# Newton-Schulz inverse: five squaring steps, or a factored geometric sum of powers

## The chip, the cores and the metric

The kernel is one program on one core of a Trainium2 chip. The metric is the device time of one execution in microseconds. The engines are TensorE (PE in the profile, with its weight loads as PEld), VectorE (DVE), ScalarE (ACT), GpSimd (POOL) and the DMA queues, most of them issued by SyncE (SP). Every engine executes its own instruction list in order; they are tied together by semaphores that are written out by hand.

## The reference, cut to what matters

Four residual blocks follow one another on x of shape 8 x 16 x 128 x 128 in float32 (batch, channel, row, column):

```
x = x + conv3x3(_gn(x), L0_weights) + bias        # conv A
x = x + newton_inverse(_gn(x), 5)                 # 128 matrices of 128 x 128
x = x + circular_conv3x3(_gn(x), L2_weight)       # conv C, written as an FFT
x = x + conv3x3(_gn(x), L3_K), last row/col zero  # conv D

def newton_inverse(W, 5):                         # per matrix, n = 128
    X = W^T / (max column abs sum * max row abs sum)
    5 times:  X = X (2I - W X)
```

_gn normalizes over pairs of channels and all pixels. With R = I - W X at the start, five Newton steps give X times the sum of R^k for k from 0 to 31. That sum is what both kernels compute, in different factorings.

## The kernel before, in words

One turn of the main loop (a cycle, `pe_cycle`, `dve_cycle`, ... with index i from 0 to 7) handles batch i's inverse and, beside it, convs of its neighbours: conv A of batch i+1, conv C and conv D of batch i-1. Cycles 0, 1, 6 and 7 are written out, cycles 2 to 5 are a hardware loop. The 16 matrices of a batch are four chunks of four (NMAT = 4); a chunk is one SBUF or PSUM tile of 128 x 512. A round works on two chunks, s = 0 and 1, in turn, so that TensorE has one chunk's products while the other's results are copied out.

The order of TensorE in a cycle is: transposes of the matrices and the Gram products of chunks 0 and 1 (`pe_norms`, lines 721 and 704), conv C of batch i-1 in six groups, **round 0**, conv A of batch i+1 in six groups, **round 1**, conv D of batch i-1 in six groups. A conv group is 9 matmuls (27 rows of a profile line marked x27 are three groups), and needs weights `w` and the high and low parts `d` of the window, which ScalarE (line 531, high) and VectorE (line 503, low) write.

A round before has five steps. `R` holds the residual matrix: step k squares it on TensorE (line 752), ScalarE copies the square from PSUM to the other R buffer (line 825), TensorE multiplies V with R (line 759), and VectorE adds the product to V (line 947 in step 0 with the scale, line 953 in steps 1 to 3, line 958 in step 4, which writes x2). Step 4 squares nothing; in round 0 it holds the Gram products of chunks 2 and 3 instead (line 704). A chunk thus takes 4 squarings, 5 products with V and 1 Gram.

GpSimd multiplies V by the scale before step 0 (line 1136, four instructions), and adds V to the kept x1 after step 3 (line 1128), since the last product is added to U = V + x1.

The order around the rounds is fixed by hand. Between the steps VectorE does side work for the neighbouring convs: statistics of the next windows (`win_stats_1`, `_2`, `_3`, lines 432 to 481), the square root's refinement of four small dependent instructions (lines 379 to 383), the conv weights (lines 494 to 496), and low parts. After round 1 it takes the statistics of x2 (line 553), on which the weights of conv C hang, while x2 goes to DRAM and comes back as windows of conv C.

## Time and profile before

| what | value |
|---|---|
| median of 3 runs | 698.43 us (694.57 to 700.22) |
| profiled execution: its span from first to last instruction | 696.2 us |
| TensorE busy | 621.8 us, 89% |
| VectorE busy | 543.7 us, 78% |
| ScalarE busy | 280.2 us, 40% |
| GpSimd busy | 198.3 us, 28% |
| one cycle of the loop, start of round 0 to the next | 78.3 us |

The profiled execution has no separate time in the results beside its span; the span lies 2.2 us under the median of the runs. In the timeline a row is start, duration, engine, line, operation, the tiles out<-in, and in brackets the idle time before it with what ended it. Rows of one kind that follow closely are merged (x4), and then the duration is that of the whole. A float32 matmul is counted as two rows in PE, so that one product of a chunk (four matmuls) is x8.

### The profile page before, as it was taken

Reading aid. Unit: us, or ns where it says so; the run is one execution under the profiler, and the core shown is the slowest. Engines: PE = TensorE matmul, PEld = TensorE weight load, DVE = VectorE, ACT = ScalarE, POOL = GpSimd, SP = SyncE. Lnnn points to the kernel's source line nnn. Section 1 sums busy time; section 2 is a strip of 40 time slices with the busy share of each in tenths; the row PEclk is TensorE's granted clock in tenths of the full one; section 3 lists DMA queues with packets and bytes.
Section 4 is the critical chain, followed back from the end, with each engine's and each line's share of the span. In section 5 each row is a group of like instructions: output and inputs, shape, how many; then the busy total and the mean of one; then the engine's idle time right before and its main releaser. Section 6 shows DMA issues by size and latency. Waiting matters only on the chain.

```text
span 696.2 us, 13213 instructions
## 1 busy us (share of the span) xinstructions
PE 621.8 (89%) x4136; PEld 530.7 (76%) x4136; DVE 543.7 (78%) x1582; ACT 280.2 (40%) x489; POOL 198.3 (28%) x299
## 2 busy tenths in 40 slices
PE   0596895999999999999999999999999999989756
PEld 0365895889779887889779887889779887987544
DVE  3866788888998797988988798987998689478560
ACT  0252222534264345424255245534264345324432
POOL 6026223440424231340414231340423041211202
PEclk9998997999999999999999999999999999999888
DMA  5131033341325414441315414441314214400432
GB/s 153 50 92 43 16 79 115 78 127 53 108 69 122 121 47 116 111 126 49 118 52 124 120 38 124 112 125 49 117 53 93 76 44 126 102 31 33 128 97 61
DMA packets 82837, 60.85 MB, mean 87 GB/s; under 512 B 8238, under 2 KB 75982, under 8 KB 81870
## 3 DMA queue, kind: packets, MB, share of 16 engines
q1 hardware_dynamic: 78558, 54.80, 28.9%
q0 software_dynamic: 4224, 5.43, 3.1%
q8 instruction: 21, 0.34, 0.2%
q14 instruction: 34, 0.28, 0.1%
HBM read 23.46 MB, written 16.91 MB: 58 GB/s over the span
## 4 chain that ended last, share of the span: by engine, by line
PE 56%; DVE 17%; SPq 12%; issue 7%; DMA 5%; ACT 2%; DVEq 0%; POOL 0%; ACTq 0%
PE conv_ps L615 30%; PE V_ps L759 11%; SPq L285 10%; PE R_ps L752 9%; DVE st L553 4%; PE R_ps L704 3%; DVE d_A L503 2%; DMA x<-out_A 2%; DVE V L953 2%; DVE x L958 2%; DMA win_C<-rows_dram 1%; SPq L271 1%; DVE dev L568 1%; SPq L318 1%; DVE sums L895 1%
## 5 line engine op out<-in xcount | busy, mean ns | idle before, releaser
L759 PE MATMUL V_ps<-V,R 128*128 128x128 f32 x1280 | 171.5, 278 | 4.3 <-DVE V L953 3.8
L759 PEld LDWEIGHTS V_ps<-V,R 128*128 128x128 f32 x1280 | 156.8, 194 | 6.5 <-DVE V L953 3.1
L752 PE MATMUL R_ps<-R 128*128 128x128 f32 x1024 | 138.3, 279 | 5.9 <-DVE R L932 5.9
L752 PEld LDWEIGHTS R_ps<-R 128*128 128x128 f32 x1024 | 126.7, 195 | 6.4 <-DVE R L932 6.4
L825 ACT ACTIVATE R<-R_ps 128x512 f32<-128x512 f32 x128 | 76.3, 596 | 121.4 <-PE R_ps L752 121.2
L615 PE MATMUL conv_ps<-d_C,w_C 128*96 128x512 f32 (+1 forms) x486 | 113.8, 388 | 10.1 <-POOL d_C L648 3.9
L1128 POOL TENSOR_TENSOR U<-V,x 128x512 f32<-128x512 f32 x32 | 42.4, 1331 | 260.5 <-DVE V L953 260.5
L615 PEld LDWEIGHTS conv_ps<-d_C,w_C 128*96 128x96 f32 x486 | 74.9, 165 | 40.3 <-issue 6.1
L615 PE MATMUL conv_ps<-d_A,w_D 128*96 128x512 f32 (+1 forms) x432 | 99.5, 385 | 4.4 <-DVE w_D L496 3.9
L615 PE MATMUL conv_ps<-d_A,w_A 128*96 128x512 f32 (+1 forms) x378 | 88.2, 389 | 4.0 <-DVE d_A L503 4.0
L615 PEld LDWEIGHTS conv_ps<-d_A,w_D 128*96 128x96 f32 x432 | 66.8, 164 | 29.9 <-DVE w_D L496 4.0
L953 DVE TENSOR_TENSOR V<-V_ps,V 128x512 f32<-128x512 f32 x96 | 65.9, 687 | 24.6 <-PE V_ps L759 21.1
L615 PEld LDWEIGHTS conv_ps<-d_A,w_A 128*96 128x96 f32 x378 | 59.1, 166 | 26.0 <-DVE w_A L496 4.0
L637 ACT ACTIVATE out_D<-conv_ps,col_D 96x508 f32<-96x508 f32 (+1 forms) x48 | 30.9, 645 | 77.4 <-PE conv_ps L615 77.4
L648 POOL TENSOR_TENSOR d_C<-d_C,ones_all 128x8 fp32r<-128x8 f32 (+1 forms) x96 | 26.1, 311 | 124.6 <-DVE d_C L503 124.6
L637 ACT ACTIVATE out_A<-conv_ps,col_A 96x512 f32<-96x512 f32 (+1 forms) x42 | 27.3, 649 | 83.2 <-PE conv_ps L615 83.2
L637 ACT ACTIVATE out_C<-conv_ps,col_C 96x512 f32<-96x512 f32 (+1 forms) x48 | 31.1, 648 | 52.6 <-PE conv_ps L615 52.6
L553 DVE BATCH_NORM_STATS2 st<-x 128x6 f32<-128x256 f32 x128 | 44.6, 412 | 9.8 <-DMA x<-out_A 9.5
L1136 POOL TENSOR_TENSOR U<-V,scl 128x512 f32<-128x512 f32 x32 | 37.8, 1210 | 37.4 <-DVE scl L922 37.4
L947 DVE SCALAR_TENSOR_TENSOR V<-V_ps,scl,U 128x128 f32<-128x128 f32 x128 | 35.9, 343 | 13.0 <-PE V_ps L759 12.8
L1107 POOL TENSOR_TENSOR DN<-x,tB 128x512 f32<-128x512 f32 x32 | 37.4, 1197 | 12.2 <-DVE dev L569 12.2
L932 DVE SCALAR_TENSOR_TENSOR R<-R_ps,scl,cst 128x128 f32<-128x128 f32 x128 | 35.2, 344 | 0.3
(173 smaller groups left out, 736.3 us busy)
## 6 DMA issues: line engine op xcount, KB each, us to landing
win_C<-rows_dram SPq DMA_DIRECT2D x40, 256.0 KB, 4.0
rows_dram<-x SPq DMA_DIRECT2D x32, 256.0 KB
y<-out_D SPq DMA_DIRECT2D x160, 48.0 KB
win_D<-out_C SPq DMA_DIRECT2D x7, 1056.0 KB, 6.8
x<-out_A SPq DMA_DIRECT2D x139, 48.0 KB
win_A<-x SPq DMA_DIRECT2D x84, 64.0 KB
win_A<-x POOLq DMA_DIRECT2D x56, 64.0 KB, 3.0
win_D<-out_C SPq DMA_DIRECT2D x14, 160.0 KB, 5.8
```

Of the source, the lines that this page charges most:

```text
L285: eng.dma_start(x1[OUT_ROWS * k:OUT_ROWS * (k + 1), :, :], out[:, k, :])\
L553: ins = dve.bn_stats(st[:, g, :], rows[:, GC * g:GC * (g + 1), :])
L615: ins = pe.matmul(conv_ps[g % 2][0:OP, 0:kn, :], c.w[:, wp, dx * OP:(dx + 1) * OP], c.d[:, dp, k0:k0 + kn, dx:dx + W], start=n == 0, stop= ...
L637: act.activation(c.out[:, k0:k0 + kn, 0:wn], conv_ps[g % 2][0:OP, 0:kn, 0:wn], ACT.Identity, bias=col(c, OUTB, rows=OP)).then_inc(c.s_out, 1)
L752: ins = pe.matmul(R_ps[s][:, m, :], Rk[:, m, :], Rk[:, m, :], start=True, stop=True)
L759: ins = pe.matmul(V_ps[s][:, m, :], Rk[:, m, :], V[ch][:, m, :], start=True, stop=True)
L825: act.activation(R[s][(k + 1 + r) % 2][:, :, :], R_ps[s][:, :, :], ACT.Copy).then_inc(s_R, 1)
L947: ins = dve.scalar_tensor_tensor(V[ch][:, m, :], V_ps[s][:, m, :], scl[:, 3, NMAT * ch + m:NMAT * ch + m + 1], U[ch][:, m, :], ALU.mult, A ...
L953: dve.tensor_tensor(V[ch][:, :, :], V_ps[s][:, :, :], V[ch][:, :, :], ALU.add).then_inc(s_V, 1)
L1107: pool.tensor_tensor(DN[:, NMAT * ch:NMAT * (ch + 1), :].rearrange("p (g a) w -> p g (a w)", a=GC), x1[:, NMAT * ch:NMAT * (ch + 1), :].re ...
L1128: pool.tensor_tensor(U[ch][:, :, :], V[ch][:, :, :], kept[:, NMAT * ch:NMAT * (ch + 1), :], ALU.add).then_inc(s_U, 1)
L1136: pool.tensor_tensor(U[ch][:, :, :], V[ch][:, :, :], scl[:, 2, NMAT * ch:NMAT * (ch + 1)].unsqueeze(2) .broadcast_to([128, NMAT, 128]), AL ...
```

## The change

The geometric sum is factored. With y = R^2, the sum of R^k for k up to 31 is (1 + R) (1 + y + ... + y^15), and the second factor is 1 + (y + y^2 + y^3)(1 + (y^3 + y^6)(1 + y^6)). Per chunk TensorE now makes y (tile RY), y^2 (RY2), y^3 (RZ) and y^6 (RZ2) in `pe_square` and `pe_power`, each copied out by ScalarE, and applies R, y^6, y^3 + y^6 (written into RX) and y + y^2 + y^3 (RC) to V in `pe_square` and `pe_apply`: 4 + 4 products and 1 Gram. The sum y^3 + y^6 is a new VectorE addition (`dve_powers`), the other one is two new GpSimd additions per chunk (`pool_powers`). VT is a new tile for V while it is multiplied; V itself stays as it was after step 0, so that GpSimd's addition of V and x1 can follow step 0.

The side work of VectorE, ScalarE and GpSimd stands in other places. In round 1, two groups of conv D are now between the applications, and the statistics of x2 are asked for later in conv D.

```diff
-STEPS = 5
+POWERS = 4
+APPLIED = 4
...
+        def pe_square(pe, b, r):
...
+                products(pe, R_ps[s], RX[s], RX[s], s_Rp)
+                products(pe, V_ps[s], RX[s], V[ch], s_Vp)
+
+        def pe_power(pe, b, r, k):
+
+            for s in range(2):
+                pe.wait_ge(s_R, at(per_R, b, n_R(r, k - 1, s)))
+                products(pe, R_ps[s], (RY, RY, RZ)[k - 1][s], (RY, RY2, RZ)[k - 1][s], s_Rp)
+
+        def pe_apply(pe, b, r, j):
+
+            for s in range(2):
+                ch = 2 * r + s
+                if j == 1:
+                    pe.wait_ge(s_R, at(per_R, b, n_R(r, POWERS - 1, s)))
                 else:
+                    pe.wait_ge((s_E, s_C3)[j - 2], at(NCHK, b, ch + 1))
+                pe.wait_ge(s_V, at(per_V, b, n_V(r, j - 1, s)))
+                products(pe, V_ps[s], (RZ2, RX, RC)[j - 1][s], V[ch] if j == 1 else VT[s], s_Vp)
...
+            for j in range(1, APPLIED):
+                pe_apply(pe, i, 1, j)
+                if prev and j < 3:
+                    conv_group(pe, cD, i - 1, j - 1, beside)
...
+        def dve_powers(dve, b, r):
+
+            for s in range(2):
+                dve.wait_ge(s_R, at(per_R, b, n_R(r, 3, s)))
+                dve.tensor_tensor(RX[s][:, :, :], RZ[s][:, :, :], RZ2[s][:, :, :], ALU.add).then_inc(s_E, 1)
...
+            dve_step(dve, i, 0, 0, 0)
+            dve_step(dve, i, 0, 0, 1)
...
+            if nxt and prev:
+                win_stats_3(dve, cA, i + 1)
+                win_weights(dve, cA, i + 1)
+                for g in range(2, 5):
+                    low_parts(dve, cA, i + 1, g)
+            dve_powers(dve, i, 0)
+            dve_step(dve, i, 0, 1, 0)
+            dve_step(dve, i, 0, 1, 1)
...
+        def pool_powers(pool, b, r):
+
+            for s in range(2):
+                ch = 2 * r + s
+                pool.wait_ge(s_R, at(per_R, b, n_R(r, 1, s)))
+                pool.tensor_tensor(RC[s][:, :, :], RY[s][:, :, :], RY2[s][:, :, :], ALU.add).then_inc(s_half, 1)
+            for s in range(2):
+                ch = 2 * r + s
+                pool.wait_ge(s_half, at(NCHK, b, ch + 1))
+                pool.wait_ge(s_R, at(per_R, b, n_R(r, 2, s)))
+                pool.tensor_tensor(RC[s][:, :, :], RC[s][:, :, :], RZ[s][:, :, :], ALU.add).then_inc(s_C3, 1)
...
-            if prev:
-                y_column(pool, i - 1)
-            pool_add(pool, i, 0)
-            pool_add(pool, i, 1)
```

VectorE in round 0 of cycle 1, before, from the end of step 0 on (col_A is a column of scalars of conv A, scaled_A and w_A its weights, d_A its low parts, V_ps the product of V in PSUM):

```order
L947 SCALAR_TENSOR_TENSOR V<-V_ps,scl,U 128x128 x8
L481 TENSOR_SCALAR col_A<-win_ps 128x1
L379 RECIPROCAL col_A<-col_A 128x1
L380 TENSOR_TENSOR col_A<-col_A 128x1
L381 TENSOR_TENSOR col_A<-col_A 128x1
L382 TENSOR_SCALAR col_A<-col_A 128x1
L383 TENSOR_TENSOR col_A<-col_A 128x1
L953 TENSOR_TENSOR V<-V_ps,V 128x512
L494 SCALAR_TENSOR_TENSOR scaled_A<-base_A,col_A,cst 128x288
L495 CAST w_A<-scaled_A 128x288
L496 TENSOR_TENSOR w_A<-scaled_A,w_A 128x288
L953 TENSOR_TENSOR V<-V_ps,V 128x512
```

The same place now:

```order
L388 TENSOR_TENSOR col_A<-col_A 128x1
L499 SCALAR_TENSOR_TENSOR scaled_A<-base_A,col_A,cst 128x288
L500 CAST w_A<-scaled_A 128x288
L501 TENSOR_TENSOR w_A<-scaled_A,w_A 128x288
L508 SCALAR_TENSOR_TENSOR d_A<-win_A,col_A,d_A 128x4x128 x3
L994 TENSOR_TENSOR RX<-RZ 128x512 x2
L982 TENSOR_TENSOR VT<-V_ps,V 128x512 x2
L508 SCALAR_TENSOR_TENSOR d_A<-win_A,col_A,d_A 128x2x128
L982 TENSOR_TENSOR VT<-V_ps,V 128x512 x2
```

Weights and three low parts of conv A, which stood between four additions to V, now stand ahead of the sums RX and of the first addition VT.

GpSimd in a full cycle, from the scaling of V on, before:

```order
L1136 TENSOR_TENSOR U<-V,scl 128x512 [waits scales_ready] x4
L648 TENSOR_TENSOR out_D<-out_C,ones_all 96x22 [waits out_C_ready]
L1128 TENSOR_TENSOR U<-V,x 128x512 [waits V_ready] x2
L271 DMA win_A<-x 128x1x128 [waits dl_A_ready]
```

and now:

```order
L1185 TENSOR_TENSOR U<-V,scl 128x512 [waits scales_ready] x4
L1165 TENSOR_TENSOR U<-V,x 128x512 [waits V_ready] x2
L1173 TENSOR_TENSOR RC<-RY 128x512 [waits R_ready] x2
L1178 TENSOR_TENSOR RC<-RC,RZ 128x512 [waits R_ready,y_plus_y2_ready] x2
L653 TENSOR_TENSOR out_D<-out_C,ones_all 96x22 [waits out_C_ready]
```

Four additions are new in each round, and the two of V and x1 follow the scaling at once, since V is final after step 0.

TensorE in round 1 of cycle 1 from the second half of the powers on, now (R_ps and V_ps are PSUM tiles, conv_ps with w_D is conv D):

```order
L750 MATMUL R_ps<-RZ 128x128 x8
L750 MATMUL V_ps<-V,RZ 128x128 x8
L620 MATMUL conv_ps<-d_A,w_D 96x512 x9
L750 MATMUL V_ps<-VT,RX 128x128 x8
L620 MATMUL conv_ps<-d_A,w_D 96x512 x9
L750 MATMUL V_ps<-VT,RC 128x128 x8
L591 MATMUL row_ps<-st,ones_mean 128x16
```

Two of the six groups of conv D, which before all followed the last product of the round, are now ahead of it.

## Rows read from the trace of the kernel before

**Rows 1.** The page, part 1: span, and TensorE's share of it.
```profile
span 696.2 us, 13213 instructions
...
PE 621.8 (89%) x4136; PEld 530.7 (76%) x4136; DVE 543.7 (78%) x1582; ACT 280.2 (40%) x489; POOL 198.3 (28%) x299
```

**Rows 2.** Windows view of one cycle: us, busy of each engine, TensorE clock, DMA.
```profile
365.70:444.00 78.30, 75.85 (x520) 64.78 (x518) 66.88 (x196) 34.69 (x62) 23.02 (x34) 1.00 0.35 96
```

**Rows 3.** Timeline of TensorE over the same cycle: start, us, engine, operation.
```profile
365.70 1.14 PE L752 MATMUL R_ps<-R 128*128 128x128 f32 x8
...
383.57 6.57 PE L615 MATMUL conv_ps<-d_A,w_A 128*96 128x512 f32 x27
...
395.68 1.05 PE L752 MATMUL R_ps<-R 128*128 128x128 f32 x8
...
411.20 2.02 PE L759 MATMUL V_ps<-V,R 128*128 128x128 f32 x16
...
430.03 2.32 PE L615 MATMUL conv_ps<-d_C,w_C 128*96 128x512 f32 x9
...
435.75 2.34 PE L615 MATMUL conv_ps<-d_C,w_C 128*96 128x512 f32 x9 [1.09 <-DVE d_C L503]
...
444.04 1.14 PE L752 MATMUL R_ps<-R 128*128 128x128 f32 x8
```

**Rows 4.** The chain that ended last: one product of a chunk on it.
```profile
366.84 0.89 PE V_ps L759 x8
```

**Rows 5.** Groups of instructions: ScalarE's copy of a power, VectorE's addition to V.
```profile
L825 ACT ACTIVATE R<-R_ps 128x512 f32<-128x512 f32 x128 | 76.3, 596 | 121.4 <-PE R_ps L752 121.2
...
L953 DVE TENSOR_TENSOR V<-V_ps,V 128x512 f32<-128x512 f32 x96 | 65.9, 687 | 24.6 <-PE V_ps L759 21.1 <-DVE col_A L383 0.9 <-DVE base_C L988 0.8
```

**Rows 6.** Timeline of GpSimd, VectorE and ScalarE in that cycle's round 0.
```profile
365.41 4.95 POOL L1136 TENSOR_TENSOR U<-V,scl 128x512 f32<-128x512 f32 x4 [4.35 <-DVE scl L922]
...
368.39 2.29 DVE L947 SCALAR_TENSOR_TENSOR V<-V_ps,scl,U 128x128 f32<-128x128 f32 x8
...
371.22 0.16 DVE L380 TENSOR_TENSOR col_A<-col_A 128x1 f32<-128x1 f32 x1
...
372.78 0.51 DVE L494 SCALAR_TENSOR_TENSOR scaled_A<-base_A,col_A,cst 128x288 f32<-128x288 f32 x1
...
374.64 0.74 DVE L503 SCALAR_TENSOR_TENSOR d_A<-win_A,col_A,d_A 128x512 fp32r<-128x512 f32 x1
...
370.89 0.71 ACT L531 ACTIVATE d_A<-win_A,col_A 128x512 fp32r<-128x512 f32 x1
```

**Rows 7.** Timeline of VectorE in round 1: window statistics for conv A.
```profile
400.49 1.47 DVE L432 BATCH_NORM_STATS2 bn_A<-win_A 128x6 f32<-128x384 f32 x3
...
403.86 0.22 DVE L412 SCALAR_TENSOR_TENSOR col_A<-mv_A,cst,col_A 128x1 f32<-128x1 f32 x1
```

**Rows 8.** Timeline where GpSimd and VectorE work at once, in two places.
```profile
411.13 2.49 POOL L1128 TENSOR_TENSOR U<-V,x 128x512 f32<-128x512 f32 x2 [24.03 <-DVE V L953]
...
411.94 0.50 DVE L565 TENSOR_TENSOR dev<-st,tB 128x16 f32<-128x16 f32 x1
412.47 1.19 DVE L568 SCALAR_TENSOR_TENSOR dev<-dev 128x16 f32<-128x16 f32 x1
...
80.23 1.42 POOL L1128 TENSOR_TENSOR U<-V,x 128x512 f32<-128x512 f32 x1 [11.31 <-DVE V L953]
...
80.55 1.41 DVE L995 TENSOR_TENSOR base_D<-base_D,scaled_D 128x288 f32<-128x288 f32 x1
```

**Rows 9.** TensorE after a pause, in the last cycle: timeline, and a window.
```profile
617.21 1.16 PE L752 MATMUL R_ps<-R 128*128 128x128 f32 x8 [1.82 <-DVE R L932]
...
618.00:620.00 2.00, 2.00 (x14) 2.00 (x13) 2.00 (x6) 0.60 (x1) 0.00 (x0) 0.60 0.00 0
```

**Rows 10.** Timeline of VectorE from the last part of x2 to conv C's low parts.
```profile
415.92 0.68 DVE L958 TENSOR_TENSOR x<-V_ps,U 128x512 f32<-128x512 f32 x1
...
427.85 1.42 DVE L503 SCALAR_TENSOR_TENSOR d_C<-win_C,col_C,d_C 128x512 fp32r<-128x512 f32 x2
```

More of the change, by code:

```diff
@@ L187, in build @@
         pick = sb("pick", [128, 2, G])
-        R = [[sb(f"R{s}{j}", [128, NMAT, 128]) for j in range(2)] for s in range(2)]
+        RX, RY, RY2, RZ, RZ2, RC, VT = ([sb(f"{n}{s}", [128, NMAT, 128]) for s in range(2)]
+                                        for n in ("RX", "RY", "RY2", "RZ", "RZ2", "RC", "VT"))
         V = [sb(f"V{ch}", [128, NMAT, 128]) for ch in range(NCHK)]
@@ L736, in pe_norms, with products @@
                               start=True, stop=True).then_inc(s_nB, 1)
[L738 removed]
+        def products(pe, out, lhsT, rhs, done):
+            for m in range(NMAT):
+                ins = pe.matmul(out[:, m, :], lhsT[:, m, :], rhs[:, m, :], start=True, stop=True)
+            ins.then_inc(done, 1)
+        def pe_square(pe, b, r):
             for s in range(2):
                 ch = 2 * r + s
[L742 to L760 removed]
@@ L765, in pe_cycle @@
                 win_var(pe, cA, i + 1)
-            for k in range(STEPS):
-                pe_step(pe, i, 0, k)
+            pe_square(pe, i, 0)
+            for k in range(1, POWERS):
+                pe_power(pe, i, 0, k)
+            for j in range(1, APPLIED):
+                pe_apply(pe, i, 0, j)
+                if j < 3:
+                    pe_gram(pe, i, j + 1)
             for g in range(NG):
@@ L837, in act_cycle @@
             act_norms(act, i, prev, nxt)
-            for k in range(STEPS - 1):
+            for k in range(POWERS):
                 act_step(act, i, 0, k, 0)
@@ L843, in act_cycle @@
                     high_parts(act, cA, i + 1, 3)
[L844 to L848 removed]
+            if nxt and prev:
+                high_parts(act, cA, i + 1, 4)
+                high_parts(act, cA, i + 1, 5)
+            keep_x1(act, i)
             for g in range(NG):
@@ L851, in act_cycle @@
                     conv_out(act, cA, i + 1, g)
+                if nxt and prev and g >= 3:
+                    high_parts(act, cD, i - 1, g - 3)
                 if nxt and prev and g == 4:
                     win_sqrt(act, cD, i - 1)
-            for k in range(STEPS - 1):
+            for k in range(POWERS):
                 act_step(act, i, 1, k, 0)
                 act_step(act, i, 1, k, 1)
-                if prev:
-                    if k == 2 and not nxt:
-                        win_sqrt(act, cD, i - 1)
-                    if k >= 1:
-                        high_parts(act, cD, i - 1, 2 * k - 2)
-                        high_parts(act, cD, i - 1, 2 * k - 1)
+                if k == 2 and not nxt:
+                    win_sqrt(act, cD, i - 1)
+            for g in range(NG):
+                if prev and not (nxt and g < 3):
+                    high_parts(act, cD, i - 1, g)
             for g in range(NG):
@@ L1063, in dve_cycle @@
-            if not prev:
+                win_stats_1(dve, cD, i - 1, 0, 1, 2)
+            dve_step(dve, i, 1, 0, 0)
+            dve_step(dve, i, 1, 0, 1)
+            if not nxt:
+                win_stats_2(dve, cD, i - 1)
+                win_stats_3(dve, cD, i - 1)
+                win_weights(dve, cD, i - 1)
+            if prev:
+                low_parts(dve, cD, i - 1, 0)
+                low_parts(dve, cD, i - 1, 1)
+            if nxt2:
+                win_stats_1(dve, cA, i + 2, 1, 2)
@@ new lines, in dve_cycle @@
+            dve_powers(dve, i, 1)
+            dve_step(dve, i, 1, 1, 0)
+            dve_step(dve, i, 1, 1, 1)
+            if prev:
+                low_parts(dve, cD, i - 1, 2)
+            if nxt:
+                dve.wait_ge(s_x1, x1_moved(i + 2))
+                if not prev:
+                    dve.wait_ge(s_x1_pool, 2 * 16 * n_x1_pool)
+                row_stats_1(dve, x1, sB_bn, 0)
+            dve_step(dve, i, 1, 2, 0)
+            dve_step(dve, i, 1, 2, 1)
+            if nxt:
+                row_stats_1(dve, x1, sB_bn, 1)
@@ L1064, in dve_cycle @@
+            if prev:
+                low_parts(dve, cD, i - 1, 3)
+            dve_step(dve, i, 1, 3, 0)
+            dve_step(dve, i, 1, 3, 1)
+            if nxt:
                 link_B = Chain(dve, s_chainB, perB, i + 1)
@@ L1068, in dve_cycle @@
             row_stats_1(dve, x2, sC_bn, 0)
+            if prev:
+                low_parts(dve, cD, i - 1, 4)
             if nxt:
```

170 lines of the change are left out of this document (61 added, 109 removed).

## The prediction

> **What bounds the kernel now.** I read the page's totals first. TensorE is busy for 89% of the span [rows 1], and 75.85 of 78.3 us in a cycle of the loop, at the full clock [rows 2]. So a cycle is TensorE's list plus 2.5 us of waits, and the question for any change is which products go and which waits come. Then I cut one cycle by TensorE's timeline [rows 3], with P the start of round 0, S the start of round 1, T the end of the last product, C the start of conv C:
>
> - P to conv A: 383.57 - 365.70 = 17.9 us. It holds 20 products of 0.89 us [rows 4], which is 17.9: no wait at all.
> - conv A: 395.68 - 383.57 = 12.1 us, about 2.2 us for a full group.
> - S to T: T is 411.20 + 2 x 0.89 = 413.0, so 17.3 us for 18 products (16.1 us) and 1.2 us of waits.
> - T to C: 430.03 - 413.0 = 17.0 us, conv D and the transposes and Grams of the next batch.
> - C to the next P: 14.0 us, with a wait of 1.1 us for conv C's third group.
>
> ScalarE's copy of a power takes 0.60 us and VectorE's addition to V 0.69 [rows 5]. Both hide now because each chunk has two products per step (R and V) and the other chunk two more.
>
> **What is removed.** Per chunk 5 + 4 products become 4 + 4. That is 4 products per cycle, 4 x 0.89 = 3.6 us, 28.6 us over eight cycles, if nothing takes its place. Of VectorE's six additions to V in steps 1 to 3 of a round four are left, and two sums RX come. Such a sum of two SBUF tiles of 512 has no row. Its bounds are 0.51 us, an instruction on 288 elements, and 0.74 us, a low part of 512 [rows 6]; I take 0.65, near the addition of 512 in rows 5. Either end moves the sum by 0.2 us per round.
>
> **What is added: a longer chain in round 0.** The powers have no products with V between them. One chunk needs 0.89 + 0.60 us and two handovers, about 1.8 us, and two chunks give TensorE 1.8 us of work, so this alone costs 0.1 us per power. But ScalarE still makes a square root and a high part between y and y^2, and ends them at 370.89 + 0.71 = P+5.9 [rows 6]. The copies of y^2 end at P+6.4 and P+7.0, where TensorE is free at P+5.4: 1 us of wait. y^6 is copied at P+10.9, the product with it ends at P+12.0, and the Gram behind it at P+12.9.
>
> The next product wants RX and VT from VectorE, and ahead of them now stand the refinement, conv A's weights and three low parts. Step 0 of V ends at 368.39 + 2.29 = P+5.0 [rows 6]. Alone, the list would take 1.3 us for the refinement and 1.3 for the weights (370.68 to 372.78 and on to 374.64, less an addition to V in each, rows 6), 2.0 for the low parts (0.67 each in sequence), 1.3 for RX and 0.6 for VT: P+11.5 or so. The last of the low parts needs a high part which ScalarE makes only after the last copy, at P+11.6, which makes it P+14.2.
>
> **What is added: the meeting with GpSimd.** Before, GpSimd has nothing after its scaling (365.41 + 4.95 = P+4.7, rows 6) until V is final. Now six additions follow at once. The rows show what happens when both engines work: VectorE's L565 waits until GpSimd's first addition ends and then takes nothing (411.94 + 0.50 = 412.44; the first of two ends at 411.13 + 1.25), and L568, which comes right after, waits out all of the second one: 1.19 us, to 413.66 [rows 8]. An addition of two SBUF tiles of 288 takes 1.41 us, to 81.96, beside a GpSimd addition that ends at 81.65 or sooner [rows 8], where the similar instruction of rows 6 takes 0.51. So the two take turns by whole instructions. The Trainium skill's page "SBUF — State Buffer" (Who interferes with whom) says the same of VectorE instructions with two SBUF inputs against a GpSimd one that reads SBUF, and exempts those with one SBUF input; by that rule the additions from PSUM stay free, as I take them; no row here speaks against it.
>
> Walked with 1.25 us per addition, from P+4.7: additions 1 to 4 end at P+5.9, 7.2, 8.4 and 9.7, and each of the four small dependent instructions of the refinement (0.16 us alone, rows 6) waits for one of them. The scaled weights wait for addition 5 (P+11.0) and end at P+11.4; the sixth addition waits for them and ends at P+12.7. Cast and low weights end at P+13.5, three low parts at P+15.5, RX at P+16.7, the first VT at P+17.3. TensorE then does 2 products, a Gram, and its pair of last products (the Gram and V's copies overlap): 5 x 0.89 = 4.5, so conv A starts at P+21.9. **Round 0: +4.0 us.**
>
> The skill's "GPSIMD Engine Reference" (4.1, Engine selection) speaks against this deal: elementwise work belongs on VectorE, GpSimd being about twice as slow for two inputs. The rows have 1.25 against 0.69 us, a factor of 1.8. With a factor of 2 an addition would be 1.38 us as an estimate by that page, and the whole sum 12 us larger; the rows are used.
>
> TensorE stands still for 4.4 us before that VT. After a pause of 1.8 us it ran at the lower of its two clock levels, mean 0.60 in the window after [rows 9]. Bounds for this are 0 and 2.4 us per pause (5 us at half clock); the nearest row gives 4 us at about 0.58, that is **+1.7 us**.
>
> **Round 1.** The same meeting: V's step 0 ends at S+5.0, two low parts follow (1.3), window statistics of 2.9 us without the addition between them [rows 7], RX and VT: S+11.2 alone. The six GpSimd additions run from S+4 to S+12.9, and low parts, the two last statistics instructions and RX each meet one. I get the first VT at S+14.5. TensorE has its products with y^6 done at S+10.8 and a conv D group until S+13.0, waits 1.5, then 2 products, a group and 2 products: T = S+20.3. Of this 4.4 us is conv D, moved. **+3.0 us**.
>
> **T to C.** The conv D work left is 7.7 us, transposes and Grams 3.6: 11.4 us. But conv C hangs on x2. From x2's last part (415.92 + 0.68 = 416.6) to the low parts of two conv C groups (429.27) VectorE has 12.7 us now [rows 10]. It gains the four small instructions of x1's row statistics, which now follow x2 (0.9 with their handovers, as estimated from the 0.2 us steps of the refinement), and two half additions' worth of meetings with GpSimd's DN (0.9), and loses a low part (0.7): 13.8 with rounding. x2's last part comes at T+1.6 (before T+3.6). So C is T+15.4 instead of T+17.0: **-1.6 us**, and TensorE waits 3.6 to 4 us here, although it had 4.4 us less to do. Its clock will fall here too, but that lies beside the next wait. Conv C's third group comes 6.5 us after those low parts in VectorE's order (435.75 - 429.27), where it now comes 5.7 after C: **+0.75**.
>
> SP's queue and GpSimd's DMA issues keep their order and count; a longer cycle gives them more room, so I cost them at nothing. If the cycle became shorter instead, the x1 rows that conv A's outputs are moved into would be late first, since VectorE's row statistics wait for them.
>
> **Sum.** 4.0 + 1.7 + 3.0 - 1.6 + 0.75 = +7.9 us per cycle, +47 in the six cycles 1 to 6. Cycles 0 and 7 lack one or two convs. In cycle 0 ten weight-building instructions stand ahead of RX, in cycle 7 the conv D statistics, so both meet GpSimd as well; between 0 and 8 us each I take 6. 696.2 + 47 + 12 = 755. The median of the runs is 2.2 us above this span: **757 us**.
>
> **The rivals.**
>
> 1. *The engines hardly meet* (GpSimd loses the races, or its additions fall into gaps). For it: the scaling beside two low parts lasts only 4.95 us. Against: every row above in which both want SBUF. Then round 0 ends at P+18.8 (+0.9, from ScalarE's high part and VectorE's order), T is S+18.7 (+1.4), C is T+14.6 (-2.4), and +0.75: +0.65 a cycle, about 704 us. Chance 0.13, the time between 697 and 712.
> 2. *The products pay.* If VectorE's chain after x2 is shorter than I sum, C comes at T+12, where TensorE's own work ends; with round 0 at P+18.8 a cycle is about 75.5, -2.9 us, in all -23: 675 us. It decides where that chain, 13.8 us, falls below 11. Against: it is 12.7 already. Chance 0.09.
> 3. *One round only.* In round 1 the conv D groups cover VectorE, since there the refinement stands before step 0; the clock stays full. +4.0 + 1.4 - 2.4 + 0.75 = +3.75 a cycle, 8 cycles: 728 us, from 715 to 735. Chance 0.12.
>
> My forecast has 0.66, with its own range 735 to 780: the low end without the clock term and with nothing for cycles 0 and 7, the high end with the clock lost in round 1 as well. **Range 706 to 780 us**: it takes in rival 3 and the upper part of rival 1 and leaves out less than 2 in 10. A measurement of this kernel tells about 1% (7 us) from no change. Faster 0.09, within 1% 0.11, slower 0.80.
>
> **What would show it.** In the changed profile: GpSimd additions with VectorE's L385 to L388 at 1 us instead of 0.16; a pause of TensorE of 4 us before its first product with VT in round 0, ended by VectorE, and a clock below 1.00 after it; round 0 near 22 us or more; C at T+15 with TensorE waiting for VectorE or GpSimd on d_C; GpSimd busy for some 280 us. The prediction is wrong if the refinement stays at 0.16 us per instruction while GpSimd adds, or if the pause before VT is under 2 us.

## The result, and the profile after

| | median | runs |
|---|---|---|
| before | 697.85 us | 4, 694.57 to 700.22 |
| changed | 740.92 us | 4, 736.92 to 743.25 |

The ratio is 1.061, with a 95% interval from 1.056 to 1.067: 43 us slower. The forecast was 757 us, with a range from 706 to 780. In the text below a cycle goes, as in the prediction, from P (start of round 0) over S (start of round 1), T (end of the last product) and C (start of conv C) to the next P.

The page of the changed kernel, its first part: the span and the busy time of each engine. It answers to [rows 1].

```profile
span 738.0 us, 12742 instructions
...
PE 618.3 (84%) x3880; PEld 521.3 (71%) x3880; DVE 594.1 (81%) x1582; ACT 280.9 (38%) x489; POOL 282.5 (38%) x363
```

TensorE has 256 rows less and is busy for only 3.5 us less. VectorE has exactly as many instructions as before and is busy for 50 us more. So the 50 us are longer instructions, not more of them. GpSimd has 84 us more; its 64 new additions, four in each of 16 rounds, are some 80 of them at 1.25 us each.

The windows view of one cycle, and of two short stretches in it (columns: us; busy PE, PEld, DVE, ACT, POOL; TensorE clock, DMA share, GB/s). It answers to [rows 2].

```profile
384.27:467.69 83.42, 75.91 (x488) 63.81 (x487) 73.52 (x196) 34.79 (x62) 33.47 (x42) 0.96 0.33 89
402.00:404.00 2.00, 2.00 (x12) 2.00 (x11) 1.11 (x2) 0.00 (x0) 1.44 (x3) 0.50 0.66 188
404.00:406.00 2.00, 2.00 (x14) 2.00 (x14) 0.00 (x0) 0.00 (x0) 0.00 (x0) 0.67 0.34 91
```

The cycle took 83.4 us instead of 78.3. In TensorE's timeline of this cycle these rows cut it, as [rows 3] did before:

```profile
384.27 1.14 PE L750 MATMUL R_ps<-RX 128*128 128x128 f32 x8
...
390.70 2.05 PE L750 MATMUL R_ps<-RY 128*128 128x128 f32 x16 [0.83 <-ACT RY L855]
...
400.53 2.56 PE L750 MATMUL V_ps<-VT,RX 128*128 128x128 f32 x16 [3.11 <-DVE VT L982]
...
406.64 6.58 PE L620 MATMUL conv_ps<-d_A,w_A 128*96 128x512 f32 x27
...
418.76 1.05 PE L750 MATMUL R_ps<-RX 128*128 128x128 f32 x8
...
432.75 2.05 PE L750 MATMUL V_ps<-VT,RX 128*128 128x128 f32 x16 [0.75 <-DVE VT L982]
...
438.53 0.29 PE L591 MATMUL row_ps<-st,ones_mean 128*128 128x16 f32 x2
...
453.78 3.55 PE L620 MATMUL conv_ps<-d_C,w_C 128*96 128x512 f32 x9 [2.74 <-POOL d_C L653]
...
467.69 1.14 PE L750 MATMUL R_ps<-RX 128*128 128x128 f32 x8
```

Round 0 took 406.64 - 384.27 = 22.4 us, conv A 12.1, S to T 438.53 - 418.76 = 19.8, T to C 15.25, C to P 13.9. Two waits carry it: 3.1 us for VectorE's VT, after which the first pair of products takes 2.56 us instead of 2.05 at a clock of 0.50, and 2.7 us for d_C, after which conv C's first group takes 3.55 us instead of 2.3.

Why VT is late stands in VectorE's timeline of the same round, beside GpSimd's:

```profile
388.41 2.49 POOL L1165 TENSOR_TENSOR U<-V,x 128x512 f32<-128x512 f32 x2
390.87 2.49 POOL L1173 TENSOR_TENSOR RC<-RY 128x512 f32<-128x512 f32 x2
393.31 2.71 POOL L1178 TENSOR_TENSOR RC<-RC,RZ 128x512 f32<-128x512 f32 x2
```

```profile
389.79 1.13 DVE L385 TENSOR_TENSOR col_A<-col_A 128x1 f32<-128x1 f32 x1
390.95 1.19 DVE L386 TENSOR_TENSOR col_A<-col_A 128x1 f32<-128x1 f32 x1
392.18 0.15 DVE L387 TENSOR_SCALAR col_A<-col_A 128x1 f32<-128x1 f32 x1
392.37 1.00 DVE L388 TENSOR_TENSOR col_A<-col_A 128x1 f32<-128x1 f32 x1
393.40 1.49 DVE L499 SCALAR_TENSOR_TENSOR scaled_A<-base_A,col_A,cst 128x288 f32<-128x288 f32 x1
394.93 1.26 DVE L500 CAST w_A<-scaled_A 128x288 fp32r<-128x288 f32 x1
396.22 0.46 DVE L501 TENSOR_TENSOR w_A<-scaled_A,w_A 128x288 fp32r<-128x288 f32 x1
```

Before, such a small instruction took 0.16 us and the scaled weights 0.51 [rows 6], and the cast 0.31, in VectorE's timeline of the kernel before:

```profile
373.32 0.31 DVE L495 CAST w_A<-scaled_A 128x288 fp32r<-128x288 f32 x1
```

GpSimd's six additions end at about 389.7, 390.9, 392.1, 393.4, 394.7 and 396.0, and five of the instructions end right behind the last five of them (390.92, 392.14, 393.37, 394.89, 396.19): each waits for an addition to end, and GpSimd's next addition gets in before the next of them. L387 alone does not wait. Behind the sixth addition L501 takes its own 0.46 us again.

This cycle is one of two kinds. Round 0 takes 22.3 to 22.4 us in four of the six cycles 1 to 6, and 20.8 us in the other two. There the wait for VT is as long, but TensorE's clock stays at 1.00 behind it (timeline of cycle 2):

```profile
236.32 2.05 PE L750 MATMUL V_ps<-VT,RX 128*128 128x128 f32 x16 [3.14 <-DVE VT L982]
```

### The profile page after: what moved, and what is told of

Same layout as the page of the kernel before. It is cut to its first block, busy times and chain, and to the rows that moved or that the text cites. A ratio compares the mean times of both kernels' runs of the same rounds, so it can differ in the third digit from the quotient of the medians.

```text
span 738.0 us, 12742 instructions
## 1 busy us (share of the span) xinstructions
PE 618.3 (84%) x3880; PEld 521.3 (71%) x3880; DVE 594.1 (81%) x1582; ACT 280.9 (38%) x489; POOL 282.5 (38%) x363
## 4 chain that ended last, share of the span: by engine, by line
PE 53%; DVE 27%; issue 10%; POOL 3%; SPq 2%; DMA 2%; ACT 1%; DVEq 1%; POOLq 0%; ACTq 0%
PE conv_ps L620 32%; PE V_ps L750 11%; PE R_ps L750 7%; DVE d_A L508 3%; DVE RX L994 3%; DVE VT L982 2%; POOL DN L1144 2%; DVE bn_A L437 2%; DVE V L976 2%; DVE st L558 1%; PE R_ps L713 1%; DVE scaled_A L499 1%; SPq L276 1%; DVE w_A L500 1%; DMA win_C<-rows_dram 1%
## 5 line engine op out<-in xcount | busy, mean ns | idle before, releaser
L620 PE MATMUL conv_ps<-d_C,w_C 128*96 128x512 f32 (+1 forms) x486 | 120.8, 406 | 24.7 <-POOL d_C L653 23.4
L620 PEld LDWEIGHTS conv_ps<-d_C,w_C 128*96 128x96 f32 x486 | 79.5, 174 | 57.4 <-issue 15.8
L750 PE MATMUL R_ps<-RY 128*128 128x128 f32 x512 | 62.1, 277 | 5.0 <-ACT RY L855 5.0
L750 PE MATMUL V_ps<-VT,RX 128*128 128x128 f32 x256 | 39.6, 318 | 30.6 <-DVE VT L982 30.6
L855 ACT ACTIVATE RY<-R_ps 128x512 f32<-128x512 f32 x64 | 37.3, 593 | 72.0 <-PE R_ps L750 72.0
L750 PEld LDWEIGHTS R_ps<-RY 128*128 128x128 f32 x512 | 59.5, 192 | 6.1 <-ACT RY L855 6.1
L750 PEld LDWEIGHTS V_ps<-VT,RX 128*128 128x128 f32 x256 | 36.5, 227 | 35.0 <-DVE VT L982 18.1
L982 DVE TENSOR_TENSOR VT<-V_ps,V 128x512 f32<-128x512 f32 x64 | 41.8, 680 | 11.8 <-PE V_ps L750 11.7
L855 ACT ACTIVATE RZ<-R_ps 128x512 f32<-128x512 f32 x64 | 38.2, 598 | 25.0 <-PE R_ps L750 25.0
L508 DVE SCALAR_TENSOR_TENSOR d_A<-win_D,col_D,d_A 128x512 fp32r<-128x512 f32 (+1 forms) x48 | 42.6, 904 | 1.8 <-ACT d_A L536 1.7
```

The costliest lines, as they stand in the source:

```text
L508: dve.scalar_tensor_tensor(c.d[:, 1, k0:k0 + kn, 1:W + 1], c.win[:, k0:k0 + kn, :], col(c, MEAN), c.d[:, 0, k0:k0 + kn, 1:W + 1].bitcast(f32),
L620: ins = pe.matmul(conv_ps[g % 2][0:OP, 0:kn, :], c.w[:, wp, dx * OP:(dx + 1) * OP], c.d[:, dp, k0:k0 + kn, dx:dx + W], start=n == 0, stop= ...
L750: ins = pe.matmul(out[:, m, :], lhsT[:, m, :], rhs[:, m, :], start=True, stop=True)
L855: act.activation((RY, RY2, RZ, RZ2)[k][s][:, :, :], R_ps[s][:, :, :], ACT.Copy).then_inc(s_R, 1)
L982: dve.tensor_tensor(VT[s][:, :, :], V_ps[s][:, :, :], V[ch][:, :, :], ALU.add).then_inc(s_V, 1)
```

## The experiments

They were measured in three groups, each beside the kernel before, whose median was 698.2, 698.4 and 698.3 us. e3 and e4 ran twice, e5 six times, the others four times. The last column is the mean of five cycles, from TensorE's window product for conv A ahead of P (`win_ps<-col_A`) in cycle 1 to the one in cycle 6, divided by five. Line numbers of the experiments differ by a few from those of the kernel that they change.

| kernel | median, us | ratio to before, 95% | a cycle, us |
|---|---|---|---|
| before | 698.3 | | 77.8 |
| changed | 740.9 | 1.061 (1.056 to 1.067) | 83.0 |
| e1, GpSimd's sums left out | 703.3 | 1.008 (1.006 to 1.010) | 79.0 |
| e2, the sums on VectorE | 724.3 | 1.038 (1.035 to 1.041) | 82.1 |
| e3, conv D unsplit | 764.0 | 1.094 (1.092 to 1.096) | 86.0 |
| e4, before with GpSimd additions | 725.0 | 1.038 (1.036 to 1.040) | 81.9 |
| e5, GpSimd's order | 704.6 | 1.009 (1.006 to 1.012) | 79.0 |
| e6, and round 0's order | 692.8 | 0.991 (0.987 to 0.994) | 77.0 |
| e7, and rows B moved | 685.3 | 0.980 (0.974 to 0.985) | 75.3 |
| e8, before with rows B moved | 706.6 | 1.010 (1.006 to 1.013) | 79.2 |
| e9, unsplit with early rows | 755.9 | 1.083 (1.078 to 1.087) | 85.3 |
| e10, e7 with the old GpSimd order | 714.7 | 1.025 (1.021 to 1.029) | 79.0 |
| e11, e7 with two additions first | 684.9 | 0.983 (0.979 to 0.987) | 75.6 |

### e1: GpSimd's sums of powers left out

```diff
-                products(pe, V_ps[s], (RZ2, RX, RC)[j - 1][s], ...)
+                products(pe, V_ps[s], (RZ2, RX, RZ)[j - 1][s], ...)
-                pool.tensor_tensor(RC[s][:, :, :], RY[s][:, :, :], RY2[s][:, :, :], ALU.add)...
+                pool.tensor_tensor(RC[s][:, 0, 0:1], RY[s][:, 0, 0:1], RY2[s][:, 0, 0:1], ALU.add)...
```

The two +y3 sums are cut to one element in the same way.

> The changed kernel with GpSimd's four sums per round cut to one element each; the last application uses y^3 in place of y + y^2 + y^3, so those sums are left out of the result. All products, copies, waits and orders stay. Theory (GpSimd's additions make VectorE's small and two-input instructions wait for whole instructions): two of six meetings are left in round 0; the third refinement step, the scaled weights and the cast get back 0.85, 1.0 and 0.95 us, the first VT comes 2 us sooner (then the last low part's high part limits it), TensorE's pause of 3.1 us falls to about 1 and its clock stays at 1.00: round 0 22.2 to about 18.8 us, round 1 shorter by 0.7 us, about -4 us per cycle, 705 us. Rival (the longer dependent chain and the order of VectorE and ScalarE cost the time, the meeting little): at most -1 us per cycle, 730 to 740 us.

Measured: 703.3 us, close to the theory's 705. VectorE's timeline of the round that starts at 366.38 shows what is left of the meeting, and what stands behind it:

```profile
371.89 1.14 DVE L385 TENSOR_TENSOR col_A<-col_A 128x1 f32<-128x1 f32 x1
373.07 0.16 DVE L386 TENSOR_TENSOR col_A<-col_A 128x1 f32<-128x1 f32 x1
...
373.64 0.52 DVE L499 SCALAR_TENSOR_TENSOR scaled_A<-base_A,col_A,cst 128x288 f32<-128x288 f32 x1
374.19 0.31 DVE L500 CAST w_A<-scaled_A 128x288 fp32r<-128x288 f32 x1
...
377.98 0.75 DVE L508 SCALAR_TENSOR_TENSOR d_A<-win_A,col_A,d_A 128x512 fp32r<-128x512 f32 x1 [1.66 <-ACT d_A L536]
378.65 1.29 DVE L994 TENSOR_TENSOR RX<-RZ 128x512 f32<-128x512 f32 x2
379.85 1.28 DVE L982 TENSOR_TENSOR VT<-V_ps,V 128x512 f32<-128x512 f32 x2
```

One instruction meets one addition and costs 1 us, the rest run as before. Now VectorE waits for ScalarE's high part, and the sums stand behind it. The first VT ends at about P + 14.2, round 0 takes 18.7 us.

### e2: the sums on VectorE

```diff
+        def dve_sums(dve, b, r):
+            for s in range(2):
+                dve.tensor_tensor(RC[s], RY[s], RY2[s], ALU.add)...
+            for s in range(2):
+                dve.tensor_tensor(RC[s], RC[s], RZ[s], ALU.add)...
...
-            pool_powers(pool, i, 0)
```

The sums stand behind VectorE's first pair of VT.

> The changed kernel, complete, with the sums y + y^2 + y^3 on VectorE right behind its first two additions VT of each round, none on GpSimd. Theory of the meeting: the four sums take VectorE 2.5 us per round where TensorE has a Gram or a conv D group beside them, and the meetings go: round 0 at 19.6 us (22.2 now), round 1 0.5 us shorter, about -3.3 us per cycle, 712 us. Rival (VectorE is already the bound, so any work moved onto it costs its length): +2.5 us per round for -1 us of meetings, 750 us or more.

Measured: 724.3 us. Neither number; 17 us better than the changed kernel, 12 worse than the theory. The refinement is free again but for one instruction. TensorE's timeline shows the price that was mis-sized:

```profile
392.55 2.05 PE L750 MATMUL V_ps<-VT,RX 128*128 128x128 f32 x16 [1.07 <-DVE VT L982]
...
396.55 2.05 PE L750 MATMUL V_ps<-VT,RC 128*128 128x128 f32 x16 [1.05 <-DVE VT L982]
```

The four sums (2.5 us) are not wholly covered: the second pair of VT stands behind them, and the last products of both rounds wait for it (1.05 us here, 0.76 in round 1). Round 1's x2 and all behind it come later too: S to T is 19.8 us and T to C 16.0.

### e3 and e9: conv D whole behind round 1

e3:

```diff
                 pe_apply(pe, i, 1, j)
-                if prev and j < 3:
-                    conv_group(pe, cD, i - 1, j - 1, beside)
...
-            for g in range(2, NG):
+            for g in range(NG):
```

> The changed kernel with all six conv D groups behind round 1, as before. Theory: the split moves work from behind x2 to ahead of it without gain or loss; unsplit, TensorE waits some 3 us for VT in round 1 and 0 to 1 us at conv C, S to C stays at 35 us: 735 to 745 us, with a lower clock in round 1. Rival (the split took the cover from the chain behind x2 and is where the time went): the wait of 2.7 us at conv C goes and nothing takes its place, 718 us.

Measured: 764.0 us, above both. The statistics of x2 stayed behind conv D's fifth group, so they moved two groups away from T, and conv C still waited 2.74 us for d_C; T to C was 19.3 us. That mixes two things, so e9 takes them apart:

```diff
-                if prev and nxt and g == 2:
+                if prev and nxt and g == 0:
                     row_var(pe, sB_bn, sB_sum, i + 1)
-                if g == 4:
+                if g == 2:
                     row_mean(pe, sC_bn, sC_sum, i)
-                if g == 5:
+                if g == 3:
                     row_var(pe, sC_bn, sC_sum, i)
```

> The changed kernel with conv D whole behind round 1, as in e3_conv_d_unsplit, and now TensorE also takes the sums of x2's statistics behind conv D's third and fourth group (two groups earlier than in e3, as in the kernel before). Theory (in e3 the wait of 2.7 us ahead of conv C came from those sums standing too late; round 1 without conv D's groups between its products still waits for VectorE's VT): e3's 764 us less 2.7 us in each of seven cycles, about 745 us: slightly above the changed kernel's 741, so that dealing conv D between the products is worth little by itself. Rival (the split is worth nothing and TensorE's order costs nothing): 735 us or less. Rival (the split is what carries round 1): 755 us or more.

Measured: 755.9 us. The split is what carries round 1. Without it TensorE waits in the middle of the round, and its clock can fall. In this cycle of e9 (timeline of TensorE, then the window over it) a pair of products takes 3.78 us instead of 2.05:

```profile
443.98 3.78 PE L750 MATMUL V_ps<-VT,RX 128*128 128x128 f32 x16 [2.85 <-DVE VT L980]
447.55 3.12 PE L750 MATMUL V_ps<-VT,RC 128*128 128x128 f32 x16
```

```profile
444.00:447.00 3.00, 3.00 (x14) 3.00 (x15) 3.00 (x7) 0.00 (x0) 0.00 (x0) 0.50 0.00 0
```

The theory had given back the whole wait ahead of conv C, but it only fell to 1.66 us. It had also left out what the clock takes in round 1: S to T is 20.5 us here and was 19.0 in a cycle of e3 where the clock stayed up. That happened in two of five full cycles of e9, and since TensorE's later waits are then shorter, it made them 0.8 us longer, not 1.5. Against the changed kernel e9 has 2.3 us more a cycle: that is what dealing conv D between the products is worth, so the second rival was right.

### e4: the kernel before, with six GpSimd additions

```diff
+            for n in range(6):
+                wait(pool, s_spare, at(6, i, n))
+                pool.tensor_tensor(spare, DN[:, 0:NMAT, :], DN[:, NMAT:2 * NMAT, :], ALU.add)...
```

They stand behind the scaling, once a cycle, and nobody uses their result.

> The kernel before, complete, with six additions of two SBUF tiles of 128 x 512 added on GpSimd right behind the scaling of V in each cycle; their results go to a spare tile that nothing reads. GpSimd is otherwise idle there for 9 us. Theory of the meeting: the small instructions of the refinement take 1.0 to 1.2 us instead of 0.16, the additions to V queue behind them and TensorE waits in round 0: +3 to +5 us in cycles 1 to 6, 718 to 730 us. Rival (idle GpSimd time is free): 698 us.

Measured: 725.0 us, +27 by additions that nobody waits for. Timeline of GpSimd, VectorE and TensorE in round 0:

```profile
385.57 8.19 POOL L1143 TENSOR_TENSOR spare<-DN 128x512 f32<-128x512 f32 x6
```

```profile
389.89 1.26 DVE L497 CAST w_A<-scaled_A 128x288 fp32r<-128x288 f32 x1
391.19 1.46 DVE L498 TENSOR_TENSOR w_A<-scaled_A,w_A 128x288 fp32r<-128x288 f32 x1
392.56 0.68 DVE L955 TENSOR_TENSOR V<-V_ps,V 128x512 f32<-128x512 f32 x1
```

```profile
393.30 1.53 PE L761 MATMUL V_ps<-V,R 128*128 128x128 f32 x8 [2.07 <-DVE V L955]
394.62 1.92 PE L754 MATMUL R_ps<-R 128*128 128x128 f32 x8
```

V's addition, which takes 0.68 us as always, stands behind the weights, and TensorE waits 2.1 us for it and then runs slower. It is the mechanism of the changed kernel, put into the one before. But the expectation had the meeting in the refinement, and it lies mostly in the weights: L382, L383 and L385 took 0.37, 0.16 and 0.93 us here (L385 to L388 of the changed kernel are L382 to L385 in e4), and the three weight instructions 0.82, 1.26 and 1.46. L383 did not wait: it started at 386.89, behind one addition's end (386.84) and just ahead of the next one's start (386.92). So a small instruction waits only if GpSimd's next addition gets in first.

### e5: only GpSimd's order

```diff
         def pool_powers(pool, b, r, full):
+            if r == 0 and full:
+                pool.wait_ge(cA.s_w, at(1, b + 1, 1))
...
+            pool.wait_ge(s_E, at(NCHK, b, 2 * r + 2))
...
+            pool_powers(pool, i, 0, nxt and prev)
             pool_add(pool, i, 0)
             pool_add(pool, i, 1)
-            pool_powers(pool, i, 0)
```

Round 1 has the same order, without the wait for the weights.

> The changed kernel, complete, with GpSimd's additions in another order and held back: in the six full cycles its two y+y2 sums of round 0 start only when VectorE has cast conv A's weights (w_A), its two +y3 sums only when VectorE has written both RX, and the V+x additions come last. Nothing is added or taken away on any engine. Theory (VectorE's small and casting instructions alternate with GpSimd's additions, and this puts the first VT late): the refinement falls back from 4.9 us to about 1.8 and the weights from 2.8 to 0.8, as in the run where GpSimd's sums were cut to one element; the first V_ps starts 3.5 us earlier, PE does not pause long enough for its clock to fall, round 0 is 19 to 20 us instead of 22.4, and the time is 705 to 720 us. Rival (what costs is the number of GpSimd's additions beside TensorE and VectorE's large instructions, wherever they stand; or the products wait for RC, that now comes later): 735 to 745 us, as the changed kernel.

Measured: 704.6 us, 36 of the 43 us gone by order alone, within 1.3 us of e1, where the sums were left out. So in a good place GpSimd's sums cost next to nothing; it is their place beside VectorE's small instructions and weights that costs. GpSimd works 3.3 instead of 2.5 us on its first pair, beside the low parts, and nobody waits for that:

```profile
377.19 3.30 POOL L1175 TENSOR_TENSOR RC<-RY 128x512 f32<-128x512 f32 x2 [3.64 <-DVE w_A L501]
```

### e6: the order of round 0 on three engines

```diff
-                if j < 3:
-                    pe_gram(pe, i, j + 1)
+                if j == 1:
+                    pe_gram(pe, i, 2)
+                    pe_gram(pe, i, 3)
...
-                for g in range(2, 5):
-                    low_parts(dve, cA, i + 1, g)
+                low_parts(dve, cA, i + 1, 2)
```

The other three low parts go behind VT; ScalarE's square root goes between the two copies of y2, its high part 3 behind the powers.

> As e5_gpsimd_order, and round 0 in another order on three engines: VectorE writes only one of conv A's low parts ahead of its sums and the other three between the steps of V; ScalarE takes conv A's square root between the two copies of y2 and its fourth high part after the three powers; TensorE runs both Grams of round 1 after the application of y6. Theory: what is left of round 0 in e1_gpsimd_sums_out is VectorE's wait of 1.7 us for ScalarE's high part d_A ahead of the sums, so the first VT comes at about P+11 instead of P+14 and round 0 takes 16.5 to 17.5 us: 3 to 5 us less than the changed kernel in each of six cycles, 20 to 30 us, and with e5's part 685 to 700 us in all. Rival (round 0 is as long as its sums, steps and copies on VectorE and ScalarE, in whatever order): within 5 us of e5_gpsimd_order.

Measured: 692.8 us. Round 0 took 377.92 - 361.43 = 16.5 us, without any wait of TensorE:

```profile
374.27 1.95 PE L750 MATMUL V_ps<-VT,RX 128*128 128x128 f32 x16
376.11 2.05 PE L750 MATMUL V_ps<-VT,RC 128*128 128x128 f32 x16
377.92 6.59 PE L620 MATMUL conv_ps<-d_A,w_A 128*96 128x512 f32 x27
...
424.43 4.12 PE L620 MATMUL conv_ps<-d_C,w_C 128*96 128x512 f32 x9 [2.75 <-POOL d_C L653]
```

Round 0 and total are as the theory had them. Of the 2.2 us that round 0 gained, conv A took 0.57 back, and conv C some more in this cycle: it still waits 2.75 us, and its first group then takes 4.12 us, at the lower clock, instead of 2.3.

### e7 and e8: the end of B's rows ahead of conv C

The same edit, in e6 and in the kernel before:

```diff
             if prev:
                 low_parts(dve, cC, b - 1, 5)
+            if not (isinstance(b, int) and b == 0):
+                dve_rows_B_end(dve, Chain(dve, s_chainB, perB, b, NROW_B - 6), b)
             dve.wait_ge(s_nT, at(1, b, 1))
...
             dve_rows_C_mean(dve, link, i)
-            if nxt:
-                dve_rows_B_end(dve, link_B, i + 1)
             row_stats_3(dve, link, sC_sum, sC_ve, tC, i)
```

> As e6_order_round0, and the six small VectorE instructions that finish B's rows (1.25 us) are moved from ahead of conv C's statistics, where TensorE then waits 2.7 us for d_C, into the norms of the next image. Theory: conv C begins where VectorE's chain behind x2 ends, so it comes 1.25 us earlier in each of seven cycles: 8 us less than e6_order_round0, 676 to 692 us; less than that where the rows of the next image then come late. Rival: the chain is not what ends the wait (the transfer of the row or ScalarE's d_C is), and the time stays within 2 us of e6_order_round0.

Measured: 685.3 us, 2.0% faster than the kernel before, by an interval of 1.5 to 2.6%. TensorE's wait ahead of conv C fell from 2.75 to 1.70 us, and in this cycle the slower groups went with it:

```profile
421.02 2.33 PE L620 MATMUL conv_ps<-d_C,w_C 128*96 128x512 f32 x9 [1.70 <-ACT V L843]
```

What ends this wait is no longer VectorE's chain. By this row it is ScalarE's copy of V (L843), which stands behind two high parts of conv C, and these had waited 1.85 us for their window to arrive from DRAM. In the cycles with waits of 2.14 and 2.04 us the clock fell again, and C to P is 14.2 us there instead of 12.7.

The cycle of this row, in the windows view, has a full clock:

```profile
359.05:433.71 74.66, 72.55 (x489) 61.46 (x487) 68.62 (x196) 34.80 (x62) 35.25 (x41) 1.00 0.37 100
```

It is 74.7 us, with 72.55 us of TensorE where [rows 2] had 78.3 and 75.85. TensorE's 3.3 us less are close to the 3.6 us of removed products in the prediction: here they are at last in the time. In the mean of five cycles the gain is 2.5 us.

> The kernel before with the same six small instructions moved in the same way as in e7_rows_b_end_ahead. It tells whether the gain of that move belongs to the changed kernel or was open all along. Theory (in the kernel before TensorE still has applications to run at that point and conv C starts without a wait, its third group waits 1.1 us): 0 to 1.1 us a cycle, 690 to 698 us, most likely 694. Rival (a chain behind x2 bounds both kernels alike): 1.25 us in each of seven cycles, 689 us or less.

Measured: 706.6 us, 8 us slower: both expectations missed, and mostly for a reason that neither had. VectorE's timeline between two parts of conv C:

```profile
358.07 2.47 DVE L895 TENSOR_REDUCE sums<-DN 128x4 f32<-128x512 f32 x4 [3.69 <-issue]
```

The view of waits, of the kernel before and of e8, has this idle three times (in all, times, longest):

```profile
DVE sums L895 <- issue: 7.6, 3, 2.8
```

```profile
DVE sums L895 <- issue: 10.8, 3, 3.7
```

No semaphore explains it. Behind it conv C's third group waits 2.42 us in e8, where [rows 3] had 1.09. Cycle by cycle, e8 against before is +0.1, +2.3, +1.6, +2.8, -0.1 us: the three middle ones are those with the idle. The rest of the 2 to 3 us is small waits of TensorE behind the moved instructions, or a lower clock behind the longer wait.

In the changed kernel and in e7 this idle is absent. The DMA view says what goes with it. Between 300 and 500 us it counts 11 packets of the kind that it calls "instruction" in the kernel before, in e2 and in e8, and 12 in e4. These four kernels are the ones with the idle (1.7 to 1.9 us in e2, 2.4 to 2.6 in e4). The changed kernel and the other eight have 0 to 2 such packets there, and no such idle. So it goes with the loading of program code inside the loop, and the changed kernel loads none in that stretch. That the loading is the cause was not tested, nor why the idle is longer in e8.

Why e8 did not gain is seen in its cycles 1 and 5, which have no idle: conv C starts there without a wait, and the edit changes the cycle by 0.1 us either way. So the gain of e7 is not an old one that lay open: the edit pays only where conv C waits for VectorE.

### e10 and e11: the meeting, in the better kernel

e10 puts GpSimd's order of the changed kernel back into e7:

```diff
-            pool_powers(pool, i, 0, nxt and prev)
             pool_add(pool, i, 0)
             pool_add(pool, i, 1)
+            pool_powers(pool, i, 0, nxt and prev)
```

with both waits of e5 taken out. e11 has the same four lines and keeps the waits. Its expectation speaks of each round, but only round 0's order was changed.

> e7_rows_b_end_ahead with GpSimd's additions back in the changed kernel's order and not held: the V+x additions first, then the powers as soon as they can. It asks whether the meeting still costs in a kernel where VectorE's and ScalarE's orders are better. Theory (each small instruction of the refinement and the cast that meets an addition waits about 1 us, 3.1 us and 2.0 us in a cycle, and VectorE is what the first V_ps waits for): 5 us a cycle less the 0.6 us that VectorE waits for ScalarE there, and 1 to 1.5 us of clock where TensorE then pauses: 5 to 6 us in each of six cycles, 715 to 722 us. Rival (the new orders leave VectorE the room): 685 to 692 us.

Measured: 714.7 us, just under the theory's 715. The number is partly luck: a full cycle lost 3.6 us, less than the 5 to 6 expected, and the rest is in cycles 0, 6 and 7. One term of the theory was too large: behind the waits for VT in round 0, of 2.0 to 2.5 us, the clock stayed at 1.00 in four of five full cycles. The order costs 36 us in the changed kernel and 29 in e7.

> e7_rows_b_end_ahead with only the two V+x additions of each round put ahead of the powers, which stay held for the weights. The two additions (2.5 us) meet the refinement, no addition meets the weights. Theory (a price for each instruction that meets an addition): two or three of the refinement's instructions take 1 us each instead of 0.16, 1.7 to 2.5 us on VectorE, less the 0.6 us that it waits for ScalarE's RZ: 1.1 to 1.9 us in each of six cycles, 7 to 12 us above e7's 685, so 692 to 697. Rival (two additions there are free, the cost comes from all six together): 683 to 688.

Measured: 684.9 us, against e7's 685.3: the total is the rival's. The rows are the theory's:

```profile
362.89 0.43 DVE L385 TENSOR_TENSOR col_A<-col_A 128x1 f32<-128x1 f32 x1
363.36 1.20 DVE L386 TENSOR_TENSOR col_A<-col_A 128x1 f32<-128x1 f32 x1
```

```profile
371.01 2.05 PE L750 MATMUL V_ps<-VT,RX 128*128 128x128 f32 x16 [0.79 <-DVE VT L985]
```

Two additions lengthen two instructions, TensorE waits 0.8 us where e7 had no wait, and round 0 is 17.65 us against 16.5. Of these 1.15 us conv A gives back 0.57: its wait of 0.32 us for col_D is gone, because x, which no longer waits for U, is ready sooner, seen from conv A's start. A full cycle is 0.3 us longer. Up to the window product of cycle 1 e11 is 3.5 us shorter (129.8 against 133.3), where the additions no longer stand behind the powers either; that this is the reason was not tested. The price of 1.1 us and more was right for round 0 and wrong for the kernel, since it left out the two other places that the order touches.

## Why the prediction was right, point by point

- **The meeting in round 0** was forecast as +4.0 us, and +1.7 for the clock. Measured together in the cycle shown: 22.4 - 17.9 = 4.5. The mechanism is shown from both sides: e5 takes it away by order, e4 puts it into the other kernel. Two sizes were off. I let each of the four refinement instructions wait for an addition; L387, a TENSOR_SCALAR, did not, and the first VT came at P + 16.2 instead of 17.3. The pause was 3.1 us, not 4.4.
- **The rest of round 0**, VT at P + 14.2 without any meeting because of ScalarE's late high part, is what e1 shows: its first VT ends at P + 14.2.
- **The clock**: the stretch from 400.53 to conv A took 6.1 us, where e5's same three entries took 4.5 (383.60 to 388.09): 1.6 us against 1.7 forecast. The windows have 0.50 and 0.67 there, and e5's stretch 1.00. But the forecast had this in every cycle, and in two of six the clock did not fall, after a pause of the same 3.1 us. What decides it is not shown.
- **Round 1**: +3.0 forecast, 19.8 - 17.3 = +2.5 measured. e1 and e5 have 18.7: 1.1 us of it is the meeting, 1.4 is conv D's two groups less the saved products and waits.
- **T to C**: -1.6 forecast, 15.25 - 17.0 = -1.8 measured, with TensorE waiting 2.7 us for d_C (3.6 to 4 forecast). This is where the removed products of round 1 went: TensorE is done sooner and waits for VectorE's chain behind x2. e7, which cuts six small instructions from that chain, moves conv C by 1.05 us a cycle and more where the clock stays up.
- **C to P**: +0.75 forecast, -0.1 measured. **This step failed**, in two ways that nearly cancel. The forecast let conv C's third group wait longer than the 1.09 us of [rows 3]; that wait is gone, and with it VectorE's idle of 2.4 us ahead of L895, out of which it came. And it let the lower clock behind TensorE's wait for d_C cost nothing, as lying beside the next wait; there was no next wait, and conv C's first group took 3.55 us instead of 2.32. Where neither the wait nor the lower clock is there, C to P is 12.7 us (cycle 1 of the kernel before, the cycle shown of e7). So the -0.1 is -1.3 for the third group's wait with what follows from it and +1.2 for the clock. That the measured interval hardly moved is a coincidence of the two.
- **Cycles 0 and 7**, 6 us each by estimate: 4.7 us more at the window product of cycle 1, and 11.5 us more from there in cycle 6 to the end (186.6 against 175.2), which is cycle 7 and, at 5.1, cycle 6. So they were 4.7 and 6.4.
- **The sum**: +7.9 a cycle forecast, 5.1 measured in the cycle shown and in the mean of five (82.95 - 77.83). The 2.8 us are 1.2 of round 0 with its clock, 0.5 of round 1, 0.2 of T to C and 0.85 of C to P.
- **The rivals.** The first, that the engines hardly meet, gave 704 us: e5 measured 704.6 where they do hardly meet. The second, that the products pay, asks for a shorter chain after x2 as well: with it and a shorter round 0, e7 comes to 685. So these were right as ways in which the kernel can go. The order of GpSimd's list decides between the forecast and the first; the second needs more than that, and with it measured 685 us, not the 675 that it named.

Of the Trainium skill's page "SBUF — State Buffer" (Who interferes with whom): the rows agree that VectorE instructions with two SBUF inputs take turns with GpSimd's additions (1.13, 1.19, 1.00 us) and that V's additions from PSUM don't (0.68 us in e4). The CAST has one input and waits too (1.26 against 0.31); the same section allows that for casts. The Trainium skill's page "GPSIMD Engine Reference" (4.1, Engine selection) would have these sums on VectorE: e2 did that, in one place of VectorE's list, and is 20 us slower than e5, which leaves them on GpSimd in a better place. In this kernel the measurement decides against that rule; other places on VectorE were not tried.

## What to carry to other kernels

An instruction of 0.16 us that shares SBUF with a running GpSimd addition of 1.25 us cost up to 1.2 us here. A chain of small dependent ones pays that again each time that GpSimd's next addition gets in between: three times of four in the changed kernel, once or twice in e4. So work that is given to GpSimd is placed by what VectorE does at that time: let it wait for the end of a chain of small instructions, and give it the stretch of long ones. When fewer products bring nothing, look at what TensorE now waits for. Here the order of GpSimd's list alone took away 36 of the 43 us of loss (e5), and shortening the two chains ahead of TensorE's waits made the kernel 13 us faster than the one before (e7).
